# Attention and mixture-of-experts kernel: the first batch's query and key parts move into the layer norm, and half of its query transfers move behind the first scores

## What is computed

```python
def attn(x, Wc_down, Wq_up, Wkv_up, Wc_proj):           # 16 heads of 16, one key/value head for all
    latent = x @ Wc_down                                # 256 -> 128
    q = (latent @ Wq_up).reshape(B, T, 16, 16)
    kv = latent @ Wkv_up                                # 128 -> 32
    k, v = kv[..., :16], kv[..., 16:]
    att = einsum('bthd,bsd->bhts', q, k) / 4            # causal mask, softmax over s
    return einsum('bhts,bsd->bthd', softmax(att), v).reshape(B, T, 256) @ Wc_proj

x = x + layernorm(attn(layernorm(x)))
x = x + layernorm(moe(layernorm(x)))                    # 8 experts, one per token, 256 -> 1024 -> 256
```

## Time and profile before

| what | value |
|---|---|
| median of three runs | 1002.3 us (1002.26 to 1006.01) |
| the profiled execution's own time | 1003.18 us |
| its span, first to last instruction | 1001.3 us |
| busy in the span | PE 869.1, DVE 700.3, ACT 535.6, POOL 301.6 us |
| mean granted TensorE clock | 0.926 of full speed |
| layer norm and latent | 0 to 38.9 us |
| first `max` event on TensorE | 55.47 us |
| first scores | 78.72 us |

### The profile page before, as it was taken

One profiled execution on the slowest core, in us unless ns is written; L12 is line 12 of the kernel. 1 busy time (PEld: TensorE's weight loads), 2 busy tenths in 40 slices (PEclk: granted clock), 3 DMA queues, 4 the chain that ended last, 5 costly groups with the idle time before them and its releaser, 6 DMA issues. The chain is left out here.

```text
span 1001.3 us, 20703 instructions
## 1 busy us (share of the span) xinstructions
PE 869.1 (87%) x5630; PEld 522.3 (52%) x5631; DVE 700.3 (70%) x2447; ACT 535.6 (53%) x909; POOL 301.6 (30%) x565
## 2 busy tenths in 40 slices
PE   5768999999999999999999658851999999999994
PEld 3322333333333333333333147741999999999993
DVE  6457788888888888888886137856466666666652
ACT  3502566666666665666666513311566565656561
POOL 1201223333233322333323223313134344343311
PEclk9955999999999999999999977955899999999998
DMA  9330011111111111211000156742011001001000
GB/s 337 115 103 11 9 52 51 48 45 37 53 58 48 48 33 46 67 44 51 24 25 18 38 200 215 223 132 74 15 31 34 31 31 34 26 33 32 17 16 7
DMA packets 54739, 62.88 MB, mean 63 GB/s; under 512 B 12526, under 2 KB 45958, under 8 KB 54544
## 3 DMA queue, kind: packets, MB, share of 16 engines
q1 hardware_dynamic: 50928, 53.67, 16.1%
q0 software_dynamic: 3744, 8.40, 2.6%
HBM read 35.86 MB, written 9.55 MB: 45 GB/s over the span
## 5 line engine op out<-in xcount | busy, mean ns | idle before, releaser
L595 ACT ACTIVATE PR<-ST 128x1024 f32<-128x1024 f32 (+1 forms) x256 | 239.4, 969 | 144.0 <-PE ST L517 144.0
L648 DVE CUSTOM_DVE_ANT_0 junk<-ring,causal 128x384 bf16<-128x384 f32 (+3 forms) x512 | 222.2, 486 | 43.6 <-PE ring L486 38.1
L486 PE MATMUL ring<-K,Q 96*128 96x512 bf16 (+3 forms) x768 | 206.1, 343 | 35.1 <-DVE R L620 10.7
L651 DVE TENSOR_REDUCE MP<-ring 128x1 f32<-128x512 f32 x256 | 164.0, 681 | 36.4 <-PE ring L486 36.2
L517 PE MATMUL ST<-Q,K 99*128 99x512 bf16 (+3 forms) x768 | 181.1, 332 | 8.7 <-DMA Q<-MT 6.9
L762 POOL TENSOR_SCALAR_AFFINE_SELECT PR<-PR 128x512 f32<-128x512 f32 x96 | 61.2, 637 | 300.1 <-ACT PR L595 295.5
L1439 PE MATMUL hp<-XNT,WS 128*128 128x128 f32 x1248 | 148.5, 278 | 2.4 <-DVE XNT L1511 2.4
L1439 PEld LDWEIGHTS hp<-XNT,WS 128*128 128x128 f32 x1248 | 148.0, 195 | 4.9 <-DVE XNT L1511 3.0
L486 PEld LDWEIGHTS ring<-K,Q 96*128 96x128 bf16 x768 | 70.6, 99 | 138.3 <-DVE MP L651 37.5
L1447 PE MATMUL yp<-W2s,HT 128*128 x624 | 141.2, 379 | 0.7 <-DVE z L1523 0.7
L517 PEld LDWEIGHTS ST<-Q,K 99*128 99x128 bf16 x768 | 59.5, 98 | 138.2 <-issue 46.9
(11 more groups left out here) (173 smaller groups left out, 901.2 us busy)
## 6 DMA issues: line engine op xcount, KB each, us to landing
Q<-T SPq DMA_DIRECT2D x192, 64.0 KB, 2.6
W1s<-in_L_ffn_W_dram SPq DMA_DIRECT2D x8, 1024.0 KB, 12.1
W2s<-in_L_ffn_W_dram SPq DMA_DIRECT2D x8, 1024.0 KB, 7.3
Y<-in_L_attn_x_dram SPq DMA_DIRECT2D x8, 512.0 KB, 6.8
Y<-W1s SPq DMA_DIRECT2D x32, 128.0 KB
XQ<-in_L_attn_x_dram SPq DMA_DIRECT2D x8, 512.0 KB, 3.6
x_rows<-XQ SPq DMA_DIRECT2D x8, 512.0 KB, 7.4
W1s<-den_rows SPq DMA_DIRECT2D x15, 256.0 KB
```

Source lines behind the costliest of these rows:

```text
L486: last = pe.matmul(bank[:, at:at + w], Q[0:NR, g, i // BW, h, i % BW * P:(i % BW + 1) * P], K[b % 2][0:NR, k * NQ:k * NQ + w], start=True, ...
L595: act.activation(PR[t % RB][:, heads[0]:heads[-1] + 1, off:NQ], unit_of(ST[(NU * n + u) % 2], s), ACT.Exp, scale=SCALE).then_inc(exp_done, 1)
L648: op = dve.tensor_tensor_reduce(junk[:, done % 2, at:at + w], src, causal[:, NQ - w:NQ], 1.0, LOWEST, ALU.add, ALU.max, dst)
L651: op = dve.tensor_reduce(dst, src, AX, ALU.max)
```

## The change

It does four things.

1. The six first pieces are made inside the layer norm part. Order and place come from `FIRST_AT`: TensorE multiplies a piece and ScalarE makes part 1 in step t (t = 2: k0, q00; t = 3: k1, q01; t = 4: q10, q11), VectorE's remainder and ScalarE's part 2 follow in step t+1, GpSimd's part 3 in step t+2. They use two PSUM banks `room` and two remainder tiles, so a piece waits for the piece two places ahead of it.
2. SyncE sends the keys and the groups 0 and 1 (24 query DMAs) within the layer norm part. The groups 2 and 3 are sent in round 0 of the loop, at steps 5 and 9. The six 1 MB loads of `W1s` leave the layer norm part: one is issued at step 4 of each of the rounds 0 to 5.
3. GpSimd normalises one of the four tiles of each step; VectorE three. The memsets of `K`, `V` and `MP` follow GpSimd's first tiles.
4. ScalarE copies `xtp` to `XT` in one instruction of 1024 elements, and takes a square root of a constant at the very start.

The core of the diff:

```diff
-FIRST = ("k0", "k1", "q00", "q01", "q10", "q11")
+FIRST = ("k0", "q00", "k1", "q01", "q10", "q11")
+FIRST_AT = {2: ("k0", "q00"), 3: ("k1", "q01"), 4: ("q10", "q11")}
...
             @block.sync
             def _(sp):
...
-                for e in range(LATE):
-                    sp.dma_start(W1s[:, :, e * F:(e + 1) * F], w1_v[e]).then_inc(w1_in, 16)
+                sp.wait_ge(ones_set, 6)
+                send_keys(sp, 0, made)
+                for g in range(2):
+                    send_queries(sp, g, made)
...
             @block.gpsimd
+                for t in range(N1):
+                    pool.wait_ge(rstd, t + 1)
+                    past(pool, xt_ready, t - 1)
+                    for i in range(HT, QT):
+                        normalise(pool, t, i).then_inc(xn_pool, 1)
...
+                    for name in FIRST_AT.get(t - 2, ()):
+                        third(name)
             @block.vector
...
+                    for i in range(HT):
+                        normalise(dve, t, i).then_inc(xn_dve, 1)
+                    if t + 1 < N1:
+                        inverse(t + 1, (t + 1) % 2)
+                    for name in FIRST_AT.get(t - 1, ()):
+                        remainder(name)
             @block.tensor
...
+                    if t:
+                        down(t - 1, (t - 1) % 2)
+                    for name in FIRST_AT.get(t, ()):
+                        i, bank, _ = spot(name)
...
+                        pe.wait_ge(lt_copied, int(name[-1]) + 1)
+                        past(pe, first_left, i - 1)
+                        piece(pe, 0, name, bank).then_inc(first_ready, 1)
             @block.scalar
...
+                for t in range(N1):
+                    if t + 1 < N1:
+                        root(t + 1, (t + 1) % 2)
+                    act.wait_ge(xt_ready, t + 1)
+                    act.activation(XT[t % 2][:, :, :], xtp[t % 2][:, :, :], ACT.Copy).then_inc(xt_copied, 1)
+                    if t:
+                        latent(t - 1, (t - 1) % 2)
+                    for name in FIRST_AT.get(t, ()):
+                        i, bank, _ = spot(name)
+                        act.wait_ge(first_ready, i + 1)
+                        act.activation(parts(name)[0], bank, ACT.Copy).then_inc(first1, 1)
+                    for name in FIRST_AT.get(t - 1, ()):
+                        second(name)
...
         @block.sync
-            send_keys(0)
-            for g in range(NG):
-                send_queries(0, g)
             sends(0, EVENT_AT[0])
             for n in range(NB):
                 b, g = divmod(n, NG)
                 for s in range(len(STEPS)):
+                    if n == 0 and s in (5, 9):
+                        send_queries(sp, 2 if s == 5 else 3, lambda name, part: None)
+                    if s == 4 and n < LATE:
+                        sp.dma_start(W1s[:, :, n * F:(n + 1) * F], w1_v[n]).then_inc(w1_in, 16)
```

## The result

| | median of five runs | lowest to highest |
|---|---|---|
| kernel before | 1003.3 us | 1002.26 to 1006.09 |
| changed kernel | 994.53 us | 992.74 to 996.25 |

The ratio is 0.991, 95% interval 0.9889 to 0.9931: faster by 0.7% to 1.1%. The profiled execution of the changed kernel took 995.65 us, its span 993.9. The forecast was 990.8 with a range of 985 to 997; the measured median lies in that range, but above the main case of 988.5 to 993.5.

What follows compares the result with a forecast made beforehand. SyncE's DMA queue was taken to hold TensorE at two places in the first 79 us. From 1003.2 us profiled, minus 6.8 (first scores) and minus 4.7 (first event) gives 991.7, or 990.8 for the median; range 985 to 997.

Steps and rivals of the forecast that it cites:

- main case: Whole kernel: both gains arrive, forecast 991 us (988.5 to 993.5), given a chance of 0.62.
- What bounds the kernel: Head of the attention part: TensorE idles at two places in the first 79 us, behind SyncE's queue of DMAs.
- Place 2: First scores: the 6.88 us wait for the maxima, queued behind query DMAs of groups 2 and 3, goes; minus 6.8 us.
- Place 1: First max event: pieces and DMAs start within the layer norm part, event at 50.7 against 55.47; minus 4.7 us.
- the equal pace of the two forms says that the mode is not on, and the sum is the same by either: Layer norm steps: VectorE's tensor_scalar is not in two-port mode, so GpSimd's quarter leaves the sum unchanged.
- What is moved elsewhere: Loop rounds: later query DMAs of groups 2 and 3 and the six 1 MB loads fit into slack; cost zero.
- a new wait: Round 0: rival that queries or the second send of maxima come too late, costing 7.6 us; 998.5 us, chance 0.07.
- slower loads: Rounds' SyncE queue: rival that W1s loads each hold a send of maxima 4.6 us; 1019 us, chance 0.04.
- only place 2: Layer norm part: rival that staggered steps take 8 us, barrier at 54.5, first event gains 0.5; 995 us, chance 0.12.
- The clock: Gap before the first event: the clock falls again, and the stretch to round 0's first half keeps its length.
- a clock of 1.00 at the first event: Listed sign of being wrong, at the first event; the clock was expected to be 0.50 there.
- The sum: Whole kernel: profiled 1003.2 us minus 6.8 minus 4.7 is 991.7; forecast of the median 990.8.

Runs made afterwards that it cites:

- e1_queue_alone: Kernel before with only SyncE's order changed: query groups 2 and 3 sent in round 0 at steps 5 and 9; 996.24 us, ratio 0.993.
- e2_group1_later: Changed kernel with group 1's 12 query DMAs moved behind the barrier, ahead of the first send of maxima; 992.35 us, ratio 0.9884.
- e3_memsets_first: Changed kernel with GpSimd's six memsets of K, V and MP back ahead of its first normalised tile; 991.99 us, ratio 0.9886.
- e10_thirds_last: Changed kernel with memsets first, group 1's DMAs behind the barrier, and GpSimd's third parts of q10, q11 moved from step 6 to step 7; 989.33 us, ratio 0.986.
- e5_w1_in_stage: Changed kernel with the six 1 MB loads of W1s back in the layer norm part, ahead of the keys; 993.15 us, ratio 0.99.
- e8_three_edits: Changed kernel with group 1's DMAs behind the barrier, GpSimd's memsets first, and all four tiles of a step on VectorE; 993.78 us, ratio 0.9877.
- e6_later_and_memsets: Changed kernel with group 1's 12 query DMAs behind the barrier and GpSimd's memsets ahead of its first tile; 991.93 us, ratio 0.9889.

## Why the prediction was right where it was right, and where it was not

- **What bounds the kernel: right.** Both places were in SyncE's queue, and e1_queue_alone and e2_group1_later show it by moving DMAs and nothing else.
- **Place 2, minus 6.8: right.** 6.92 at the first scores in e1_queue_alone. In the changed kernel the distance from first event to first scores is 15.96 for the 16.4 foreseen. Half of the 0.4 is the clock, which fell 0.3 us behind the first event and not ahead of it; the kernels with the low clock there took 16.16 to 16.17, so the other half is the estimate. TensorE itself is next, as foreseen: the scores follow its event matmuls with no wait.
- **Place 1, minus 4.7: right in its mechanism, mis-sized by half.** SyncE's 24 DMAs after k1's third part set the event, as worked out. It came at 53.29 and not 50.7. The terms: step 3 began at 21.91, not 20.5 (1.4). The steps 3, 4 and 5 took 5.96, 6.69 and 5.60 (40.16 less 34.56) for the 5.5, 6.4 and 5.3 foreseen, of which the first two count for k1 (0.75). And from SyncE's last issue to the event it was 0.83, not the 0.45 that I took from a barrier at which SyncE had long been (0.4). The 1.4 is TensorE's late rise to full pace in the profiled execution, but for 0.1 that stood already at step 0: e2_group1_later, the same program up to there, rose earlier and began step 3 at 20.51. That this meets the 20.5 foreseen is luck, for it holds a cost of 0.6 that no term had, GpSimd's memsets in step 0 (e3_memsets_first). The computation ended at 49.42 for the 46.3 foreseen; it stayed ahead of SyncE, so these 3.1 us did not count here, and they set the event in the kernels with group 1 later.
- **A step that failed in it** is "the equal pace of the two forms says that the mode is not on, and the sum is the same by either". I had inferred from tensor_scalar taking no less than bn_stats that it uses no port that GpSimd shares. The row of step 0 says the opposite: 2.85 us for 1.03 of work, and 1.08 once the memsets are elsewhere. The Trainium skill ("SBUF — State Buffer", section "Who interferes with whom") has the pair of ports as a lock that whoever comes first holds for the whole instruction. I had told only the half in which VectorE shuts GpSimd out; on the path was the other half. By that rule the trace agrees: 2.85 beside the copy and the memsets, 1.88 beside third parts, 1.03 beside neither. Whether a two-port mode was on, no row shows. In the changed kernel step 6's 0.85 lay beside SyncE's issuing and cost nothing; in e10_thirds_last, where the computation sets the event, taking it away counts.
- **What is moved elsewhere, zero: right.** No wait for `Q<-T` or for `Q<-MT` stands behind the first scores of the changed kernel, and e5_w1_in_stage puts the loads at nothing. The rivals of a new wait and of slower loads are out. The rival "only place 2" had 995, next to the 994.53 measured, but not its cause: its steps of 8 us and an event at 55 did not come, and place 1 earned 2.2 us.
- **The clock: half right.** It did fall, and the part up to round 1 kept its length (44.31 from first scores, 45.04 before). But it fell at 53.6, after the gap of 4.5 us and not in it. By the prediction's own list, a clock of 1.00 at the first event was a sign of being wrong, and it was 1.00 there; it mattered little: e2_group1_later had 4.1 us of it and the changed kernel 0.3, and their distances are equal (15.95 and 15.96). And I had not seen that the clock can fall already in the staggered steps: it fell between 35 and 43 us in the nine other kernels above that make the pieces in this stage, though not in the changed kernel's profiled execution.
- **The sum.** The median came 3.7 above the forecast. 1.3 of it stands at round 1 (113.56 for 123.76 - 11.5 = 112.26). 1.0 is the kernel before itself, 1003.3 in this comparison and 1002.3 in the runs that I started from. The other 1.4 is in what follows round 1, and the trace of the profiled execution shows where most of its own 2.8 (10.20 less 7.4) went: the scores are 10.19 earlier than before up to 285.07, 9.50 earlier at 287.96, behind a wait of TensorE for VectorE, and 8.03 earlier at 293.24. In between, from 289.1 to 292.5, the clock was low. The low stretch took 1.5 us, the wait ahead of it 0.7.

```profile
289.00:290.00 1.00, 1.00 (x4) 0.20 (x2) 1.00 (x3) 0.98 (x2) 0.00 (x0) 0.56 0.11 29
290.00:291.00 1.00, 1.00 (x6) 0.20 (x8) 1.00 (x3) 1.00 (x2) 0.00 (x0) 0.50 0.55 188
```

Such a fall in the full rounds stands in three other kernels too (at 411 us in e8_three_edits, at 284 and 346 in e10_thirds_last, at 547 in e6_later_and_memsets) and in none of the rest. What brings it on is open; the wait ahead of it (1.40 us at 287.73 here) does not settle it, since such waits stand in all of them.

## What to carry to other kernels

If a queue holds up a wait at two places, its DMAs must be counted at both, and the gains of putting them later and of starting them sooner are not added up: here 6.9 us shrank to 2.4 once the start was moved, and two parts worth 6.9 and 7.6 alone were worth 9.5 together. Before giving GpSimd work beside VectorE, look at what VectorE runs at that time, and put GpSimd's memsets and subtractions beside statistics, subtractions out of PSUM or waits, which kept their pace here (four bn_stats 1.37 to 1.40 us, a subtraction 0.65 to 0.69), and not beside tensor_scalar; an even pace in a trace in which GpSimd is idle says nothing on whether the two can run side by side. When an early stage is stretched so that TensorE waits for a few microseconds in each step, reckon with a clock at the low level over what follows: it came in nine of ten executions here, 3.4 to 6.8 us long.

## What the hardware showed that I had not expected

- VectorE's tensor_scalar, float32 from SBUF to SBUF, three of 128x256: 1.03 us by itself, 2.85 beside GpSimd's copy and memsets, 1.88 beside its tensor_tensor; four: 1.35 against 3.10 to 3.33. The third parts themselves stay at 1.15 each.
- GpSimd's tensor_scalar of 128x256 float32 takes 1.22 us, against 0.34 on VectorE (1.35 / 4), and its tensor_tensor of twice the elements takes 1.15.
- TensorE's start: its matmuls run at half pace until 16.5 to 19.5 us, differently from execution to execution. Between the changed kernel and e2_group1_later, the same program up to there, that moved the start of SyncE's query DMAs by nearly all of the 1.57 us between them (0.12 stood already at step 0).
- A barrier at which SyncE arrives last, straight from issuing, takes 0.83 to 0.84 us to TensorE's first matmul (four kernels), 0.45 where ScalarE arrives last (six, the kernel before among them).
